# Masking attention scores by receiver: 128-wide one-hot rows replaced by three base-8 digits carried beside the scores

## The reference

```python
def _attention_aggregate(h_proj, sender, receiver, attn_vec, num_nodes):
    h_sender = h_proj[sender]
    h_receiver = h_proj[receiver]
    e = einsum('ehd,hd->eh', h_sender, attn_vec[:, :HD]) + einsum('ehd,hd->eh', h_receiver, attn_vec[:, HD:])
    e = leaky_relu(e, 0.2)
    e_max = segment_max(e, receiver)
    alpha = exp(e - e_max[receiver])
    alpha = alpha / (segment_sum(alpha, receiver)[receiver] + 1e-8)
    return segment_sum(h_sender * alpha[..., None], receiver)
```

## Time and profile before

| | |
|---|---|
| median of 3 runs | 3961.57 us |
| the profiled execution's own time | 3974.88 us |
| span in its profile | 3973.1 us |
| mean granted TensorE clock | 0.795 |
| PE, DVE, POOL, ACT busy | 63%, 61%, 45%, 21% |
| top pass, direction 0 and 1 | from 1888 to 2656 us, from 3257 to 3592 us |
| gather stream | from 1853 to 3194 us |
| guard pass loop, direction 0 and 1 | 2700 to 2984 us, 3634 to 3725 us |
| weighted pass, direction 0 and 1 | 2998 to 3245 us, 3740 to 3925 us |

### The profile page before, as it was taken

How to read it: one execution, slowest core, us unless ns; L and a number is a source line. 1 busy time by engine, 2 the same in 40 slices (tenths; PEclk the granted TensorE clock), 3 DMA queues, 4 the chain that set the end, 5 groups by cost and what they waited for, 6 DMA issues and landing times.

```text
span 3973.1 us, 55703 instructions
## 1 busy us (share of the span) xinstructions
PE 2520.3 (63%) x16100; PEld 1579.7 (40%) x16104; DVE 2428.8 (61%) x3420; ACT 837.5 (21%) x1390; POOL 1806.2 (45%) x2211
## 2 busy tenths in 40 slices
PE   1688777779498997753555555542225469995663
PEld 0334554544345554333322223222224455554663
DVE  8999988873512034862444444463225379999877
ACT  0396333310111012100000000001112231212442
POOL 6300333313777777202777777788777600000000
PEclk9799999989799999875665556565557699995697
DMA  1000111134253420523333334323336740000253
GB/s 60 0 0 13 45 45 41 45 103 149 51 158 71 98 43 1 126 57 67 101 95 99 97 95 93 101 84 90 95 101 193 165 115 0 0 0 0 73 176 91
DMA packets 195122, 301.59 MB, mean 76 GB/s; under 512 B 120540, under 2 KB 133818, under 8 KB 194922
## 3 DMA queue, kind: packets, MB, share of 16 engines
q1 hardware_dynamic: 138986, 175.88, 13.9%
q0 software_dynamic: 40512, 62.87, 8.8%
q10 hardware_dynamic: 15552, 61.94, 5.1%
HBM read 191.65 MB, written 88.01 MB: 70 GB/s over the span
## 4 chain that ended last, share of the span: by engine, by line
PE 47%; DVE 22%; issue 14%; another core or an unknown queue 8%; ACT 5%; DMA 2%; DVEq 1%; POOL 1%; ACTq 1%; SPq 0%; POOLq 0%; PEldq 0%
PE PS L532 11%; PE PS L1101 8%; PE PS L692 8%; PE PS L1105 7%; PE PS L879 5%; ACT arena L508 3%; DVE arena L1137 3%; DVE arena L553 3%; PE PS L968 3%; DVE arena L1194 2%; PE PS L470 1%; PE PS L955 1%; DVE arena L368 1%; PE PS L1240 1%
## 5 line engine op out<-in xcount | busy, mean ns | idle before, releaser
L532 PE MATMUL PS<-arena 128*128 128x400 f16 (+2 forms) x4320 | 796.7, 336 | 308.6 <-issue 93.3
L1296 POOL DMA_INDIRECT arena<-T_att,idx x864 | 837.3, 969 | 280.0 <-issue 177.3
L1137 DVE TENSOR_REDUCE arena<-PS 128x512 f32 (+1 forms) x864 | 555.5, 689 | 478.4 <-PE PS L1105 224.3
L532 PEld LDWEIGHTS PS<-arena 128*128 128x128 f16 (+2 forms) x4320 | 543.9, 163 | 551.1 <-issue 391.8
L1101 PE MATMUL PS<-big_id,arena 128*128 128x512 bf16 x864 | 404.4, 468 | 378.1 <-issue 213.8
L1472 POOL DMA_INDIRECT order<-arena x400 | 511.1, 1278 | 252.5 <-issue 252.5
L553 DVE TENSOR_SCALAR arena<-arena 128x1600 f16<-128x1600 f16 x448 | 385.6, 906 | 58.5 <-PE PS L532 53.4
L1105 PE MATMUL PS<-arena,pick 128*128 128x128 bf16 x3456 | 408.7, 252 | 0.0
L1105 PEld LDWEIGHTS PS<-arena,pick 128*128 128x128 bf16 x3456 | 320.3, 114 | 150.4 <-issue 84.8
L692 PE MATMUL PS<-arena 128*128 128x512 f16 (+1 forms) x1575 | 316.6, 361 | 95.4 <-issue 82.2
L627 POOL TENSOR_TENSOR rdeg<-rdeg,arena 128x1600 f32<-128x1600 f32 x48 | 160.0, 3333 | 307.2 <-ACT arena L611 307.2
(11 more groups left out here) (254 smaller groups left out, 3198.8 us busy)
## 6 DMA issues: line engine op xcount, KB each, us to landing
spill<-arena SPq DMA_DIRECT2D x108, 560.0 KB
arena<-spill ACTq DMA_DIRECT2D x108, 560.0 KB
arena<-A SPq DMA_DIRECT2D x50, 800.0 KB
A<-arena SPq DMA_DIRECT2D x50, 400.0 KB, 2.4
arena<-A SPq DMA_DIRECT2D x50, 400.0 KB
arena<-T_att,idx POOLq DMA_INDIRECT x864
order<-arena POOLq DMA_INDIRECT x400
T_att<-h SPq DMA_DIRECT2D x2, 1600.0 KB, 12.4
```

Source lines behind the costliest of these rows:

```text
L532: return t.matmul(where, lhsT, rhs, start=False, stop=True, skip_group_check=True)
L1137: v.tensor_reduce(cmax[d][:, :, bass.ds(i * SLOTS + half * GROUP + j, 1)].rearrange("p h k -> p (h k)"), PS[:, bank:bank + BANK].rearrange ...
L1296: p.indirect_dma_start(out=ring1[:, b, j, :], out_offset=None, in_=T_att[d][:, :], in_offset=bass.IndirectOffsetOnAxis(ap=idx[:, d, k:k + ...
```

## The change

A receiver number r (0 to 127), plus one, is written as three digits to base 8 (the numbers 0 to 128, so the last digit is 0, 1 or 2 and has four columns). Beside its 12 score columns each edge now carries 8 + 8 + 4 = 20 columns that are 1 where they match its digits, so `score_buf` is 28 wide (`SIGNS`). After the transpose those 20 rows lie below the 12 score rows in `sT`. `pick` gets 20 more rows: for each node, -2^100 where a digit's value is not the node's. One product per head over four chunks (512 columns, one bank) then gives scores plus mask at once. A unit is now two heads of four chunks in two banks, reduced by one DVE instruction of 1024 elements; two units are in flight instead of four banks. The digits of all edges are computed once after the keys are there; per group DVE makes the 20 columns in two small instructions that compare SBUF with SBUF. `big_id`, the product over it, the 128-wide one-hot, its semaphores `used` and `oh_ready` go.

```diff
+BASE = 8
+SIGNS = SPLIT * HEADS + 2 * BASE + BASE // 2
-        score_buf = sb("score_buf", [P, 2, GROUP, SPLIT * HEADS], BF16)
+        score_buf = sb("score_buf", [P, 2, GROUP, SIGNS], BF16)
...
-                a.copy(score_buf[:, half, :, :], sE[d][:, bass.ds(i * SLOTS + half * GROUP, GROUP), :]) \
+                a.copy(score_buf[:, half, :, 0:SPLIT * HEADS], sE[d][:, bass.ds(i * SLOTS + half * GROUP, GROUP), :]) \
...
                 t.wait_ge(scores_brought, GB[d] + 2 * i + half + 1)
-                bank = PS[0:SPLIT * HEADS, at:at + BANK].bitcast(BF16)
+                t.wait_ge(digits_ready, 2 * (GB[d] + 2 * i + half) + 2)
+                bank = PS[0:SIGNS, at:at + BANK].bitcast(BF16)
...
-                t.wait_ge(oh_ready, 2 * (SB[d] + i) + half + 1)
                 t.wait_ge(sT_ready, n + 1)
-                for j in range(GROUP):
-                    s = half * GROUP + j
-                    bank = (j % 4) * BANK
-                    t.wait_ge(reduced, n * GROUP + j + 1)
-                    t.matmul(PS[:, bank:bank + BANK], OHb[:, s, :],
-                             big_id[:, :].unsqueeze(1).to_broadcast([P, HEADS, P]), start=True, stop=False,
-                             skip_group_check=True)
-                    for hd in range(HEADS):
-                        last = t.matmul(PS[:, bank + hd * P:bank + (hd + 1) * P], pick[:, hd, :], sT[:, s, :],
-                                        start=False, stop=True, skip_group_check=True)
+                for q in range(UNITS):
+                    s = half * GROUP + q // 2 * QUAD
+                    t.wait_ge(reduced, n * UNITS + q + 1)
+                    for hd in range(q % 2 * 2, q % 2 * 2 + 2):
+                        last = t.matmul(PS[:, hd * BANK:(hd + 1) * BANK], pick[:, hd, :],
+                                        sT[:, s:s + QUAD, :].rearrange("p j e -> p (j e)"), start=True, stop=True)
                     last.then_inc(masked_ready, 1)
-                t.nop().then_inc(used[half], 1)
...
-            def others(i, half):
-
-                v.wait_ge(used[half], SB[d] + 1 + i)
+            def digits(i, half):
+
                 c = bass.ds(i * SLOTS + half * GROUP, GROUP)
-                v.tensor_tensor(OHb[:, half * GROUP:(half + 1) * GROUP, :],
-                                steps_at.unsqueeze(1).to_broadcast([P, GROUP, P]),
-                                key[:, d, c].unsqueeze(2).to_broadcast([P, GROUP, P]), ALU.not_equal) \
-                    .then_inc(oh_ready, 1)
+                to = score_buf[:, half, :, SPLIT * HEADS:]
+                v.tensor_tensor(to[:, :, 0:2 * BASE].rearrange("p j (n a) -> p j n a", n=2),
+                                low[d][:, c, :].unsqueeze(3).to_broadcast([P, GROUP, 2, BASE]),
+                                figures.unsqueeze(1).unsqueeze(1).to_broadcast([P, GROUP, 2, BASE]), ALU.is_equal) \
+                    .then_inc(digits_ready, 1)
+                v.tensor_tensor(to[:, :, 2 * BASE:], high[d][:, c].unsqueeze(2).to_broadcast([P, GROUP, BASE // 2]),
+                                figures[:, 0:BASE // 2].unsqueeze(1).to_broadcast([P, GROUP, BASE // 2]), ALU.is_equal) \
+                    .then_inc(digits_ready, 1)
...
+            def reduce(i, half, units):
+                for q in units:
+                    v.wait_ge(masked_ready, (2 * (SB[d] + i) + half) * UNITS + q + 1)
+                    u = q % 2 * 2
+                    v.tensor_reduce(cmax[d][:, u:u + 2, bass.ds(i * SLOTS + half * GROUP + q // 2 * QUAD, QUAD)],
+                                    PS[:, u * BANK:(u + 2) * BANK].rearrange("p (h k e) -> p h k e", h=2, k=QUAD),
+                                    AX_X, ALU.max).then_inc(reduced, 1)
...
+            digits(0, 0)
+            digits(0, 1)
             with v.Fori(0, ST[d] - 1) as i:
                 for half in range(2):
                     reduce(i, half, first)
-                    others(i + half, 1 - half)
+                    digits(i + 1, half)
                     reduce(i, half, second)
...
-            dve_link(v.tensor_scalar(big_id[:, :], ident, NEG_BIG, None, ALU.mult))
...
             v.tensor_scalar(k0, back_i, 8, None, ALU.arith_shift_right).then_inc(order0_ready, 1)
+            v.tensor_copy(figures, iota[:, 0:BASE])
+            for d in range(2):
+                whole = digit_i[:, 0, 0:CH[d]]
+                parts_i = digit_i[:, 1:, 0:CH[d]]
+                dve_link(v.tensor_scalar(whole, key[:, d, 0:CH[d]], 1.0, None, ALU.add))
+                v.tensor_scalar(parts_i[:, 0, :], whole, BASE - 1, None, ALU.bitwise_and)
+                v.tensor_scalar(parts_i[:, 1, :], whole, 3, BASE - 1, ALU.arith_shift_right, ALU.bitwise_and)
+                dve_link(v.tensor_scalar(parts_i[:, 2, :], whole, 6, None, ALU.arith_shift_right))
+                v.tensor_copy(low[d], parts_i[:, 0:2, :].rearrange("p n k -> p k n"))
+                dve_link(v.tensor_copy(high[d], parts_i[:, 2, :]))
             v.wait_ge(rT_summed, 1)
...
+    node = np.arange(P) + 1
+    at = SPLIT * HEADS
+    for digit, values in ((node % BASE, BASE), (node // BASE % BASE, BASE), (node // BASE ** 2, BASE // 2)):
+        other = np.where(digit[None, :] != np.arange(values)[:, None], NEG_BIG, 0.0)
+        c[at:at + values, C_PICK:C_ALL] = np.tile(other, (1, HEADS))
+        at += values
```

More of the change, by code:

```diff
@@ L119, in gnn_kernel @@
         ident_b = sb("ident_b", [P, P], BF16)
-        big_id = sb("big_id", [P, P], BF16)
         pick = sb("pick", [P, HEADS, P], BF16)
@@ L243, in gnn_kernel @@
               for a, e in ((h[:, :, :].rearrange("p t f -> p (t f)"), EDGE[0]), (W, EDGE[1]))]
-        OHb = OH[:, :, :].bitcast(BF16)[:, :, 0:P]
+        low = [W[:, at:at + c].bitcast(BF16).rearrange("p (k n) -> p k n", n=2) for at, c in ((2688, CH[0]), (3104, CH[1]))]
+        high = [W[:, at:at + c // 2].bitcast(BF16) for at, c in ((3552, CH[0]), (3760, CH[1]))]
+        digit_i = view(18816, 4 * CHUNKS).bitcast(I32).rearrange("p (n k) -> p n k", n=4)
+        figures = W[:, 3984:3984 + BASE // 2].bitcast(BF16)
         eq = OH_flat.bitcast(BF16).rearrange("p (g j e) -> p g j e", g=LAP, j=GROUP)
@@ L289, in gnn_kernel @@
         table = {n: sem(f"table_{n}") for n in ("att0", "att1")}
-        oh_ready = sem("oh_ready")
-        used = [sem(f"used{i}") for i in range(2)]
+        digits_ready = sem("digits_ready")
         round_done = sem("round_done")
@@ L1055, in gnn_kernel @@
         KEEPS = GROUP
+        QUAD = 4
+        UNITS = 2 * GROUP // QUAD
         def top_act(a, d):
@@ L1067, in take @@
                 a.wait_ge(sT_summed, 2 + GB[d] + 2 * i + half + 1)
-                bank = PS[0:SPLIT * HEADS, (4 + 2 * half) * BANK:(5 + 2 * half) * BANK].bitcast(BF16)
-                a.copy(sT[0:SPLIT * HEADS, half * GROUP:(half + 1) * GROUP, :],
+                bank = PS[0:SIGNS, (4 + 2 * half) * BANK:(5 + 2 * half) * BANK].bitcast(BF16)
+                a.copy(sT[0:SIGNS, half * GROUP:(half + 1) * GROUP, :],
                        bank.rearrange("p (j e) -> p j e", j=GROUP)).then_inc(sT_ready, 1)
@@ L1118, in top_pe @@
             mask(ST[d] - 1, 1)
-            for half in range(2):
-                t.wait_ge(used[half], SB[d] + 1 + ST[d])
+            t.wait_ge(masked_ready, UNITS * (GB[d] + GR[d]))
             t.drain().then_inc(round_done, 1)
         def top_dve(v, d):
-            def others(i, half):
-                v.wait_ge(used[half], SB[d] + 1 + i)
+            def digits(i, half):
                 c = bass.ds(i * SLOTS + half * GROUP, GROUP)
-                v.tensor_tensor(OHb[:, half * GROUP:(half + 1) * GROUP, :],
-                                steps_at.unsqueeze(1).to_broadcast([P, GROUP, P]),
-                                key[:, d, c].unsqueeze(2).to_broadcast([P, GROUP, P]), ALU.not_equal) \
-                    .then_inc(oh_ready, 1)
@@ L1133, in reduce @@
[L1133 to L1141, removed]
@@ L1143, in top_dve @@
+            first, second = range(0, UNITS // 2), range(UNITS // 2, UNITS)
+            digits(0, 0)
+            digits(0, 1)
             with v.Fori(0, ST[d] - 1) as i:
@@ L1145, in top_dve @@
                     reduce(i, half, first)
-                    others(i + half, 1 - half)
+                    digits(i + 1, half)
                     reduce(i, half, second)
-            reduce(ST[d] - 1, 0, first)
-            others(ST[d] - 1, 1)
-            reduce(ST[d] - 1, 0, second)
-            reduce(ST[d] - 1, 1, range(GROUP))
+            for half in range(2):
+                reduce(ST[d] - 1, half, range(UNITS))
         def guard_dve(v, d):
@@ L1224, in guard_pe @@
         def guard_pe(t, d):
-            t.wait_ge(reduced, 4 + CB[d] + CH[d])
+            t.wait_ge(reduced, 2 + UNITS * (GB[d] + GR[d]))
             for hd in range(HEADS):
@@ L1581, in _ @@
             v.sem_inc(scaled_ready, 1)
-            v.sem_inc(reduced, 4)
+            v.sem_inc(reduced, 2)
             v.sem_inc(er_ready, 2)
@@ L1690, in _ @@
```

(2 more changed lines are left out.)

1 line of the change is left out of this document (removed).

## The result

The changed kernel takes 3846.3 us (median of 4 runs; the longest, 3996.94, was in a slower state at a granted clock of 0.656 and the ratio leaves it out, the other three lie from 3830.92 to 3852.61) against 3962.54 us: ratio 0.9695, 95% interval 0.9658 to 0.9731, so 3.1% or some 120 us faster. Forecast were 3807 us, with 3755 to 3870 as the forecast's own range and 3900 as the reach for the next two cases. **On another chip the same pair of kernels shows no difference at all**; that is the larger lesson, and comes with the experiments.

What follows compares the result with a forecast made beforehand. No single engine bounds it: late PE signals beside POOL's stream bound direction 0's top pass, DVE direction 1's. A 150 us gain shrinks to 116 in the weighted pass and ends at 155: 3961.6 - 155 = 3807 us, range 3755 to 3870, reaching 3900.

Steps and rivals of the forecast that it cites:

- the next two cases: Whole kernel: only direction 1's top pass gains (3900 us, chance 0.12), or the weighted pass gives back (3878 us, 0.14).
- The bound of the first pass, and its end: Direction 0's top pass: bound by engine handover, then by the 11.9 us gather; ends at 2498 in place of 2656.
- the port: Direction 0's top pass: small two-SBUF-operand DVE instructions may hold POOL up; 8 us taken, 0 to 23 possible.
- A queue charged by matmul, 0.31 to 0.34 us: Top and guard passes beside POOL's stream: PE's finish signals are served slowly, at that price for each matmul.
- The other path that I set beside it: Direction 0's top pass: two turns of PE, signal and DVE after ACT's copy, 9 to 10 us a group.
- It loses its cover: Direction 0's weighted pass: all 52 groups run beside the stream, 295 us; the gain shrinks from 150 to 116.
- The second rival: Direction 0's weighted pass: at 9.7 us a group beside the stream it gives the gain back; 3878 us, chance 0.14.
- The second pass: Direction 1's top pass: 10 groups at 7 us beside the stream, 46 at 4.8, DVE-bound; end 3437 against 3592.
- run 67 us beside the stream: Direction 1's top pass: a duration, the stream stays on 67 us after its start at 3141, 10 groups at 7 us.
- the 18 us kept for the half level: Direction 1's top pass: PE at half clock would stall DVE some 0.4 us a group; in the range only.
- Only the second pass gains: Direction 0's top pass stays at 14.8 us a group, direction 1's gains 62 us; 3900 us, chance 0.12.
- A fixed delay: Top pass: signal lateness L is no queue, a group takes 5.3 + 2L; slower by 68 us, 4030, chance 0.07.

Runs made afterwards that it cites:

- the pass with 72 of them: Changed kernel with each 512-column top-pass product issued as eight of 64 columns, second chip: first top pass 630 us, kernel 3792.9 us.
- a stand-in: Changed kernel with 16 signals a group in place of 5 in the top pass, the extra ones awaited by nobody, second chip: 3705.8 us.

## Why the prediction was right, and where not

**The bound of the first pass, and its end: right.** 14.8 us a group became 11.7; the end was put at 2498 plus 8 for the port, it came at 2494. That this was handover and not an engine's work is borne out three times: by the recorded updates of the two kernels on the first chip, by holding the stream on the second, and by a chip on which the same 40 masking matmuls a group fit under the gathers. **The reason I gave for the price was wrong.** "A queue charged by matmul, 0.31 to 0.34 us" came from two stretches of one chip that happened to agree. On the second chip the guard loop costs 217 / (52 x 16) = 0.26 us a matmul, and the pass with 72 of them 0.17 at most; one number for both does not exist. What stands: the signals are late only beside the stream, fewer matmuls in the same time relieve them, the number of signals doesn't matter (tested on the second chip), and how late they are differs from chip to chip. That the forecast held in spite of this is because the new pass lay so far under the gather (5.3 against 11.8) that any price up to twice mine would have given the same end. The other path that I set beside it was added up wrongly, without effect: its own formula, 5.3 + 2L with L = 1.5, gives 8.3 us and not 9 to 10.

**The small DVE operations: sized too high.** I took 8 us for the port, with 23 as the bound. The last copy came 1.6 us later than before (2482.4 against 2480.8), and on the third chip, where both kernels ran side by side, the score copies of direction 0 span 616.2 us without and 616.3 with them, from first start to last. The 49 gathers that lie beside a small DVE operation in the changed kernel's first pass have a median of 0.96 us, as have the 379 that don't. The rule of the exclusive pair of ports (the Trainium skill, "SBUF — State Buffer", section "SBUF: two separate sides") would by the guard's rows have added up to 23 us. The large operations of the guard pass follow it; of the ones of 0.28 and 0.18 us only two score copies beside them, 0.24 and 0.27 us in place of 0.21, show a trace of it. DVE's time for them was 0.3 + 0.2 us, overlapped; the second pass at 4.83 us a group was forecast at 4.8.

**The weighted pass: right in kind, undersized.** "It loses its cover" was worth 34 us in the sum; it measured 325 us from first to last group against 244, so 81. 52 groups at 6.3 us, not 5.7. This is the largest error of the sum. Of the 39 us between 3807 and 3846, 20 are in the profile: the weighted pass took 47 more than allowed and the guard loop 9, while the first top pass gave 15 more than the forecast and the second 21. That the errors half cancel is luck. The other 19 us are the distance of the two profiled executions from their medians. I had averaged over three stretches of the old pass in which POOL paused for DMA traffic more than it did in the new place: 118 gathers in 210 us there, 0.56 a us, and 209 in 325 us now, 0.64 a us, with a DMA share of 0.73 then and 0.62 now. That the pauses are what sets the pace is argued from this, not tested. The second rival, which had this pass give the gain back, came true by half (128 us lost by it, 34 by the forecast, 81 measured): its pace of 9.7 us a group is not reached in any of four stretches of the new pass (one L1347 a group), which run at 6.2, 8.3, 5.0 and 4.9:

```profile
2843.00:2930.00 87.00, 17.01 (x14) 0.74 0.60 180
2930.00:3030.00 100.00, 14.21 (x12) 0.62 0.53 164
3030.00:3100.00 70.00, 15.76 (x14) 0.70 0.62 195
3100.00:3168.00 68.00, 15.81 (x14) 0.78 0.80 181
```

As in the old pass beside the stream, the quick stretches are those in which DMA is busiest.

**The second pass: right in its rate, wrong in its overlap.** I had it start at 3141 and run 67 us beside the stream at 7 us a group. It started at 3187, 5 us before the last copy, and ran all its groups undisturbed: 270 us, not 296. From the end of the weighted pass to the end of this one the forecast had 308 us and it took 287: the 21 us of the sum above. The granted clock was 1.00 of full in it, so the 18 us kept for the half level weren't needed.

**The rivals.** Only the second pass gains: refuted here, the first gave 164 us. A fixed delay: refuted, where DVE was waiting for a unit in the new pass it started 0.15 us (median of 52) after the unit's end. **What no case of mine held** is that the answer is the chip's: -3.1% on the first, -103 us on the second by a stand-in, -0.07% on the third, within noise. I had given no change 3 in 100. The trace of one chip couldn't speak for it: what I called the first pass's bound belonged to that chip, or to what went on around it at the time, and not to the kernel. That the measurement fell on a chip with late signals, where this forecast holds, was luck too. With prompt signals the bound is the stream from 1853 to 3200 and the change moves nothing that ends last.

## What to carry to other kernels

When one stretch runs far under the rate of every engine in it and the same instructions run at full rate elsewhere, look for late handovers, and then measure on another chip before tuning for them: the kernel before was 367 us apart on two chips, all of it in such stretches. If a stage follows a stream, ask how long the stream itself is; here one line in POOL's loop (8 small copies against one) gave 190 us with the change and 140 without it on chips with prompt signals, where 32 fewer matmuls a group by themselves gave nothing, and only then was the change worth its 55 us. A price that two stretches of one trace agree on is still one trace.

## What was not expected of the hardware

PE's signals of finished matmuls can arrive several us late while POOL streams its gathers (in the old first pass ACT started 7.3 us after the transposes' end in the median, 10.8 at most), and prompt on another chip with the same program: the kernel before took 3962, 3809, 3595 and 3600 us on four chips, the unchanged guard loop of direction 0 280 us on the first, 217 on the second, 81 on the others. PE goes on meanwhile: between 2500.53, the end of the transposes in the earlier trace rows, and ACT's start at 2509.32 it worked through four more banks, the last of them here:

```profile
2507.63 0.63 PE L1105 MATMUL PS<-arena,pick 128*128 128x128 bf16 x4
```

So the signal is late and not the work of the engine. The signals of DVE and ACT were prompt at the same time on the first chip (their updates 0.01 us after the end, 0.05 us from the end of a reduction to the next work of PE, computed from the records). On a late chip two in three or more of the gaps between late arrivals of PE's signals lie within 0.06 us of a multiple of 0.725 us, half of POOL's 1.43 us from gather to gather, so they arrive at two points of POOL's cycle; and a pause of POOL of 1.7 us lets all that are held through at once. Which part of the stream does it, these runs leave open: the ones that were to tell it ran where the signals were prompt anyway. Open is also whether the chip itself makes the difference. Each was used for a short time only, and what else ran on it is not recorded, so load from neighbouring cores is a rival that nothing here rules out; the kernel before repeats within 0.4% on each chip that ran it more than once.
